# A sparse-attention and mixture-of-experts kernel: GpSimd's descriptor scratch region is set to 4096 bytes per partition

## What is computed

```python
x = layernorm(x + L0_attn(x))   # every row attends to 96 keys: its last 64 and 32 chosen by top-k of an index score
x = layernorm(x + L0_ffn(x))    # top-1 router over 32 experts, capacity 80 rows each: scatter, expert FFN, gather
x = layernorm(x + L1_attn(x))   # nine shifted copies of x @ value_W, gated by sigmoids, layernorm with gamma and beta
x = layernorm(x + L1_ffn(x))    # 8 experts, top 2, as one masked hidden layer, plus a shared one
```

## Time and profile before

| what | value |
|---|---|
| time, median of 3 runs | 941.9 us (939.28, 941.9, 943.36) |
| profiled execution, span from its first to its last instruction | 1199.2 us |
| PE busy, with mean granted clock | 913.6 us (76%), 0.811 |
| DVE busy | 679.3 us (57%) |
| ACT busy | 509.0 us (42%) |
| POOL busy | 480.2 us (40%) |
| transfers of POOL (queue q0) | 12800 packets, 14.15 MB, 5.8% of 16 DMA engines |

### The profile page before, as it was taken

One profiled execution on the slowest core, in us unless ns is written; L12 is line 12 of the kernel. 1 busy time (PEld: TensorE's weight loads), 2 busy tenths in 40 slices (PEclk: granted clock), 3 DMA queues, 4 the chain that ended last, 5 costly groups with the idle time before them and its releaser, 6 DMA issues.

```text
span 1199.2 us, 17728 instructions
## 1 busy us (share of the span) xinstructions
PE 913.6 (76%) x5742; PEld 520.4 (43%) x5742; DVE 679.3 (57%) x1979; ACT 509.0 (42%) x1463; POOL 480.2 (40%) x738
## 2 busy tenths in 40 slices
PE   6699749289479796879676794875749897888885
PEld 3345415145245453536343352443426582343353
DVE  3788628067158466549474473884403314968763
ACT  5456315044136464547354372643416332423420
POOL 3600562712711777573717427156560104411020
PEclk8668859679579788879687697885859998988987
DMA  8101211101100111110101001001070251000000
GB/s 232 34 1 25 43 26 38 29 20 33 29 19 5 25 26 23 21 23 16 23 11 22 19 12 23 11 17 25 16 188 21 69 139 31 1 1 10 0 10 18
DMA packets 59642, 39.98 MB, mean 33 GB/s; under 512 B 27072, under 2 KB 51360, under 8 KB 59424
## 3 DMA queue, kind: packets, MB, share of 16 engines
q1 hardware_dynamic: 44064, 23.40, 7.6%
q0 software_dynamic: 12800, 14.15, 5.8%
q10 hardware_dynamic: 2688, 1.31, 0.4%
HBM read 33.31 MB, written 5.55 MB: 32 GB/s over the span
## 4 chain that ended last, share of the span: by engine, by line
PE 46%; another core or an unknown queue 20%; DVE 13%; issue 10%; ACT 8%; DMA 1%; POOL 1%; SPq 0%; DVEq 0%; ACTq 0%; POOLq 0%
PE psI L655 5%; PE psK L745 5%; PE psK L641 4%; PE psS L1753 3%; PE psP L807 3%; PE psP L814 2%; PE psS L781 2%; PE psK L733 2%; ACT R L903 2%; PE psP L796 2%; PE psS L784 2%; DVE SC L1115 2%; PE psP L641 2%; DVE G L1971 1%
## 5 line engine op out<-in xcount | busy, mean ns | idle before, releaser
L621 POOL DMA_INDIRECT G<-key_rows,idx x284 | 276.2, 973 | 349.0 <-DVEq L1142 247.8
L1031 ACT ACTIVATE PT<-psP 128x256 f32<-128x256 f32 x128 | 48.7, 380 | 360.1 <-remote 270.3
L1311 DVE CUSTOM_DVE_ANT_0 S<-psS,cst 128x208 f32<-128x208 f32 x128 | 47.4, 370 | 262.9 <-remote 225.2
L655 PE MATMUL psI<-kiT,qiT 64*128 64x512 f32 (+5 forms) x320 | 108.3, 697 | 74.1 <-ACT R L903 57.1
L641 PE MATMUL psK<-cst 128*128 128x512 bf16 x315 | 101.4, 437 | 6.3 <-issue 6.3
L781 PE MATMUL psS<-KT,Q 96*32 96x128 f32 x1024 | 64.8, 305 | 27.9 <-remote 17.5
L1115 DVE SCALAR_TENSOR_TENSOR SC<-R,w_i,SC 128x512 f32<-128x512 f32 (+5 forms) x120 | 78.5, 654 | 5.5 <-ACT R L903 1.9
L1145 DVE MAX8 top<-SC 128x8 f32<-128x128 f32 (+15 forms) x64 | 78.5, 1226 | 2.3
L1007 ACT ACTIVATE KT<-psK 96x512 f32<-96x512 f32 x96 | 56.7, 591 | 51.9 <-remote 26.4
L903 ACT ACTIVATE R<-psI 128x512 f32<-128x512 f32 (+5 forms) x160 | 73.3, 510 | 12.2 <-PE psI L655 6.0
L1147 DVE FIND_INDEX8 idxf<-top,SC 128x8 uint32<-128x128 f32 (+15 forms) x64 | 78.2, 1223 | 0.0
(11 more groups left out here) (348 smaller groups left out, 1889.1 us busy)
## 6 DMA issues: line engine op xcount, KB each, us to landing
G<-key_rows,idx POOLq DMA_INDIRECT x284
rtmp<-idx_rows SPq DMA_DIRECT2D x32, 128.0 KB
xslots<-zrow SPq DMA_DIRECT2D x4, 320.0 KB, 9.0
SC<-xslots SPq DMA_DIRECT2D x8, 160.0 KB
yslots<-SC ACTq DMA_DIRECT2D x8, 160.0 KB, 2.7
V<-val_rows SPq DMA_DIRECT2D x15, 80.0 KB
xr<-in_x SPq DMA_DIRECT2D x1, 1024.0 KB, 9.3
qiT<-in_w_gate SPq DMA_DIRECT2D x4, 256.0 KB
```

The source lines that it names most:

```text
L621: pool.indirect_dma_start(ring[o % RING][:, g % GPB, DR:], None, key_rows, bass.IndirectOffsetOnAxis(ap=idx[:, t, g:g + 1], axis=0),).then ...
L655: pe.matmul(psI[i][:, 0:w], lhs, kiT[64 * i:64 * i + 64, CH * c:CH * c + w], start=True, stop=True).then_inc(s["i_mm"], 1)
```

## The change

One argument is added where the program is made. The scratch region in which GpSimd's software writes the descriptors of its transfers is 4096 bytes in each partition, a quarter of the default. No instruction of the program is added, removed or moved.

```diff
@@ -2223,7 +2223,7 @@
-    nc = _bacc.Bacc("TRN2", target_bir_lowering=False, num_devices=1)
+    nc = _bacc.Bacc("TRN2", target_bir_lowering=False, num_devices=1, dynamic_dma_scratch_size=4096)
```

## The result

| | before | changed |
|---|---|---|
| median of the runs | 942.14 us (939.28 to 943.36, 4 runs) | 931.37 us (930.74 to 933.06, 4 runs) |
| ratio, 95% interval | | 0.9896 [0.9875, 0.9917] |

The changed kernel is faster: the medians differ by 10.8 us, and the ratio of the runs is 1.04% under 1 (7.8 to 11.8 us by its interval). The forecast was no change, 941.9 us with a range from 938.5 to 945.5, so the result lies outside it.

What follows compares the result with a forecast made beforehand. It took the chain, with PE at 46%, to bound the kernel and POOL's gathers to be covered by their distance to use; all terms added 0 to the 1199.2 us profile, giving 941.9 us, range 938.5 to 945.5.

Steps and rivals of the forecast that it cites:

- step (2): Gathers from tile 8 on: long gaps move, 7 per tile for 9, -0.6 us a tile, covered by at least 15.9 us.
- step (4): The 16 gathers of line 1540, on the chain: taking back in about four groups costs 0, at most 1.2 us.
- The ring: POOL's descriptor room: 113 transfers before, 28 after; four taken back together, 0.29 us if it shows, hidden where transfers follow directly.
- Step (1): Tiles 5 to 7: taking back starts at the 29th transfer, 2.0 us of POOL (0 to 6.4), nothing passed on.
- The scaling by 0.785: Whole kernel: profile microseconds on the chain times 0.785, the runs' median 941.9 over the profile's span 1199.2.
- Step (3): Waiting for ring room: the transfer taken back is some 40 us old, slowest landing 5.7 us, so 0.
- A: Lines 621 and 1540: ring too short, transfers wait for landings, 2.6 us a step, 1061 us; chance 0.03.
- B: Ring gives back one transfer at a time, so each gather costs 0.29 us more, 945.5 us; chance 0.05.
- C: Argument leaves the ring as it was, or its limit is in transfers; long gaps stay, 941.9 us; chance 0.05.
- D: Tensors move with the region's size, some access gets faster or slower, 932 to 951 us; chance 0.07.

Runs made afterwards that it cites:

- s2048_d: Kernel before with a scratch region of 2048 bytes (ring of 14 transfers), on the fifth chip: 936.19 us, 0.993 of before.
- s4800: Kernel before with a scratch region of 4800 bytes (ring of 33 transfers), on the fifth chip: 909.07 us, 0.965 of before.
- s13568: Kernel before with a scratch region of 13568 bytes (ring of 94 transfers), on the first chip: 1195.18 us, 0.990 of before.
- s14336_c: Kernel before with a scratch region of 14336 bytes (ring of 99 transfers), on the fourth chip: 918.98 us, 0.976 of before.
- before_d: Kernel before, unedited, run again on the fourth chip: 942.45 us, 1.001 of before.
- early16384: Kernel before with a 448-column spacer in place of 64 at every fourth gather in tiles ahead of 8, fourth chip: 938.79 us, 0.998 of before.
- pad4096: Changed kernel plus an unused tensor of 12288 bytes per partition, so tensors lie where they lay before, third chip: 1139.36 us, 0.977 of before.
- before_again: Kernel before, unedited, run again on the first chip: 1202.45 us, 1.0003 of before.

## Why the prediction was wrong

Two steps failed, and a smaller third: the cover of step (2), which isn't there at 942 us; the end of the program, for which the sum had no term; and step (4), taken at 0. What follows goes through the prediction's parts.

**The ring** was read rightly, to the transfer: 113 and 28 long, four or one taken back together, hidden where transfers follow directly, the first visible one at the 85th transfer, 7 in each tile, always the fourth gather. The time given for it, 294.4 us, was that of a chip with late updates; it came at 226.07. The same count, run over all 400 transfers with rings of 14, 28, 33, 94, 99 and 113, with block starts and scatters left out as hidden, puts a long gap (0.5 to 0.7 us) at each gather where s2048_d, the changed kernel, s4800, s13568, s14336_c and before_d show one, and at no other. By these six sizes a transfer takes between 143.7 and 144.3 bytes. The estimate worked out from the Trainium skill, DMA: Bandwidth & Descriptors, section The descriptor swizzle, whose count is of a 1 MiB transfer, and its Terms is 144 bytes for a transfer. The runs agree.

**Step (1), early taking back.** 7 showed in tile 7, 2.0 us as taken. They were hidden, as said: POOL still waits 6.4 us for tile 8's indices, and early16384 adds more there than this and loses nothing.

**Step (2), the places.** The size was right: -0.6 us a tile were 14 x 0.287 = 4.0 us in tiles 8 to 15. The stream shortened by 387.3 - 382.9 = 4.4 us. "Both are covered by at least 21.6 - 5.7 = 15.9 us of distance" is the sentence that failed. The distance was that of the earlier trace rows, taken in an execution of 1199 us, in which PE's updates came late and held up everything but POOL. At 942 us the distance at the last block is 1.5 us. "With the cover gone they would cost their full size" was in the text, but for the last tile alone. The cover is gone in tiles 13 to 15, and what tiles 8 to 12 save arrives there as well, because the stream is unbroken from 276 us to 660. Not all of the 4.4 us arrives at the end: tile 8's indices come 0.9 us later in the changed kernel's profile, the last scatter is 3.1 us earlier, the first gather of line 1540 2.8 us (730.0 against 732.8), the last output, with step (4)'s 0.9 us lost on the way, 2.1 us.

**The scaling by 0.785** failed with it. It took the span to be longer by one factor everywhere. The surplus of 257 us lay in one kind of place: the chain gave 20%, some 240 us, to another core or an unknown queue, in a program of one core. That row was read past. Taken out, it would have left about 960 us, near the 942 of the runs, and an engine that is never held up by it, POOL, would have come out with no distance.

**Step (3)** held: no gather waits for a landing of the ring. **Step (4)** failed by the sign that the prediction gave for it, over 21 us for the 16 gathers of line 1540. The changed kernel's first, sixth and last of them, with the earlier trace rows to compare, and then before_d's sixth:

```profile
730.00 1.00 POOL L1540 DMA_INDIRECT R<-yslots,slot_out  x1 [36.45 <-DMA yslots<-SC]
...
736.87 0.94 POOL L1540 DMA_INDIRECT R<-yslots,slot_out  x1 [0.86 <-DMA R<-yslots,slot_out]
...
750.57 0.95 POOL L1540 DMA_INDIRECT R<-yslots,slot_out  x1 [0.30 <-issue]
```
```profile
739.37 0.94 POOL L1540 DMA_INDIRECT R<-yslots,slot_out  x1 [0.54 <-DMA R<-yslots,slot_out]
```

From 730.00 to 751.52 are 21.5 us; before_d needs 20.6. The difference is in the three waits for the batch before, at the sixth, tenth and fourteenth gather (0.86, 0.88 and 0.92 against 0.54, 0.55 and 0.66 us), not in the 0.30 us steps. By the count of the ring the changed kernel takes back four transfers at each of these three (and at the second, which has no wait, and where nothing shows); with 113 they fall on others, where nothing shows either. So a wait seems to lay the taking back of four open as a spacer does. The other runs agree: with rings of 28 and 94, whose counts fall on the same gathers, the 16 take 21.3 to 21.6 us in four profiles, with all other sizes 20.5 to 20.9 us in sixteen. For single transfers it is less clear: with the ring of 14 the count puts one at the tenth and one at the fourteenth gather, and only the latter's gap is longer (0.74 to 0.88 us). The prediction had the number of takings back ("about four groups") and took 0 for them from the rows of before, where they lie elsewhere; it is 0.9 us, within (4)'s upper bound of 1.2.

**The missing term.** Nothing in the sum stood for the end of the program. It is 6.0 - 0.4 = 5.6 us, more than all terms that were weighed, and it doesn't need the quick chip: in the profile before, too, the last output was issued at 1190.93 and the span ended at 1199.2, 8.3 us later. s2048_d measures it almost alone: 943.6 - 936.19 = 7.4 us (4.4 to 8.9 by its interval).

With both, 2.1 + 5.6 = 7.7 us, which is the difference of the spans, 938.98 - 931.25. The medians differ by 10.8 with a lower end of 7.8; the profiled execution of the changed kernel was the slowest of its four. Of the 3 us between, 1.7 are the distance of that execution from its median, and 1.1 that of before_d's (941.0 us) from 942.14: they are spread between executions.

**The rivals.** A, B and C fell by the gaps: none is over 0.6 us but for waits of the program, not every gather has one, and they moved. D got no support from pad4096, on a chip with late updates. On a quick one it wasn't tried, but before_d and the changed kernel have the engines busy alike (DVE 678.9 and 679.2 us, ACT 508.1 and 508.3, PE 837.9 and 837.1, POOL 493.2 and 492.2), so no engine's work got shorter. The case that came true, faster through the end of the program and an exposed stream, was not among them.

## What to carry to other kernels

Before distances are read from a profile, its span is set against the times of the runs: where they differ by a quarter, find which waits make the difference, take those out, and only then ask which engine is ahead. Follow the trace to its last microsecond, past the last output, since what the program's end does is time as well. And for a kernel with many indirect transfers the length of the ring is worth a trial of several sizes: short, and such that the taking back falls where two transfers follow directly and none waits. The trial has to be made on more than one chip: 14336 bytes, which do the latter, won on one kind and lost on the other.

## What the hardware showed unexpectedly

- The same kernel takes 942 us on two chips and 1156 to 1205 on three. On the latter PE's semaphore updates come late while POOL issues gathers (L814 in before_again: median 3.2 us, 77% over 0.5 us), and a small edit can have the opposite sign: 14336 bytes are 0.976 on one kind and 1.024 and 1.049 on the other.
- On those chips longer spacers between gathers made the kernel faster, 0.926 of before with 14336 bytes.
- Between the end of the stream and the last scatter s4800 needs 26.5 us, before_d 32.4 and s14336_c 33.1. The windows over this stretch show a higher granted clock (s4800, then before_d; the last columns are PEclk, DMA share, GB/s):

```profile
642.78:669.28 26.50, 24.36 (x193) 14.95 (x192) 10.88 (x74) 14.49 (x53) 6.09 (x7) 0.94 0.15 51
```
```profile
662.91:695.31 32.40, 30.00 (x191) 18.12 (x189) 10.60 (x74) 14.61 (x53) 6.12 (x6) 0.74 0.13 42
```

PE has about the same matmuls done, 193 and 191, and is busy for 92 and 93% of the stretch in both. The clock stays at its lower level, 1.2 GHz, until 645.8 us in s4800 and until 680.0 us in before_d. The difference of 5.9 us between s4800 and before_d is more than the 3 us by which s4800 came in below its expectation; what raised the clock is open, and with it how much of s4800's lead another program would see.
